# Rounded weight pairs in the expert units, and three reorderings at stage borders of a fused attention and expert kernel

## The reference, cut to what matters

```python
x = x + L0_xattn(layernorm(x), ctx)           # attention map of 256 x 256 per batch
x = x + L0_ffn(layernorm(x))                  # 8 experts, top 2, and a shared one
x = x + L1_xattn(ctx, ctx, layernorm(x))      # masked softmax of scores * layernorm(x)
x = x + L1_ffn(layernorm(x))                  # weights looked up in a table of 16 values

def L0_ffn(xt):                               # xt: 1024 x 256
    top_p, top_i = top_k(softmax(xt @ gate_w), 2)
    for k in (0, 1):                          # an expert takes up to 160 tokens per k
        h = gelu(buf @ w1 + b1)               # 256 -> 1024
        y = h @ w2 + b2 + gelu(buf @ wd) @ wu # 1024 -> 256, and rank 32
        out += y[token's slot] * keep * top_p[:, k]
    return out + 0.2 * (gelu(xt @ sw1 + sb1) @ sw2 + sb2 + gelu(xt @ swd) @ swu)

def L1_ffn(x):                                # lut[idx] are the weights
    return (silu(x @ gate.T) * (x @ up.T)) @ down.T
```

## Time and profile before

| quantity | value |
|---|---|
| median of 3 runs | 301.19 us (301.11 to 302.14) |
| profiled execution | 304.5 us, span of its instructions 302.7 us |
| PE busy | 290.1 us (96%), 1931 instructions |
| DVE busy | 243.2 us (80%) |
| ACT busy | 155.2 us (51%) |
| POOL busy | 116.3 us (38%) |
| granted PE clock | 1.000 over the whole span |

### The profile page before, as it was taken

One profiled execution on the slowest core, in us unless ns is written; L12 is line 12 of the kernel. 1 busy time (PEld: TensorE's weight loads), 2 busy tenths in 40 slices (PEclk: granted clock), 3 DMA queues, 4 the chain that ended last, 5 costly groups with the idle time before them and its releaser, 6 DMA issues.

```text
span 302.7 us, 5910 instructions
## 1 busy us (share of the span) xinstructions
PE 290.1 (96%) x1931; PEld 251.9 (83%) x1931; DVE 243.2 (80%) x647; ACT 155.2 (51%) x369; POOL 116.3 (38%) x144
## 2 busy tenths in 40 slices
PE   8988999969999999999999999999999899999895
PEld 6545688859898998989899888999888699999795
DVE  4888878848998988889888899898974778796733
ACT  2677985415554655646556555655533634535210
POOL 7527410351328074380834706051051215442431
PEclk9999999999999999999999999999999999999999
DMA  7933206550949448293573926446034000010102
GB/s 214 333 137 88 90 0 191 176 173 2 299 166 260 175 83 305 61 298 128 133 253 69 326 93 168 171 79 226 1 43 141 0 3 0 0 36 1 36 1 70
DMA packets 21858, 38.07 MB, mean 126 GB/s; under 512 B 3147, under 2 KB 12427, under 8 KB 21836
## 3 DMA queue, kind: packets, MB, share of 16 engines
q1 hardware_dynamic: 17356, 32.55, 32.6%
q0 software_dynamic: 4480, 5.25, 9.2%
HBM read 31.37 MB, written 6.42 MB: 125 GB/s over the span
## 4 chain that ended last, share of the span: by engine, by line
PE 69%; DVE 11%; ACT 7%; DMA 5%; POOL 4%; issue 3%; SPq 0%; DVEq 0%; POOLq 0%; ACTq 0%
PE hb L811 25%; PE yb L830 24%; PE yb L845 5%; PE hb L959 4%; PE tb L711 4%; DVE bst L1231 1%; POOL rstd L472 1%; DMA xg<-xnorm_dram,row_of 1%; DMA x<-xacc_dram 1%; DVE xn L1237 1%; PE rb L976 1%; DMA xacc_dram<-ysb,third_row 1%; PE yb L959 1%; ACT sm L1024 1%; DMA projw<-projw_dram 1%
## 5 line engine op out<-in xcount | busy, mean ns | idle before, releaser
L830 PE MATMUL yb<-raw,h 128*128 128x256 f32 x384 | 96.5, 379 | 1.4 <-ACT h L1137 1.4
L830 PEld LDWEIGHTS yb<-raw,h 128*128 128x128 f32 x384 | 69.1, 189 | 8.8 <-ACT h L1137 1.8
L1137 ACT ACTIVATE h<-hb,b 128x320 f32<-128x320 f32 (+1 forms) x80 | 44.6, 558 | 58.4 <-PE hb L811 57.1
L811 PE MATMUL hb<-xT_hi,w_hi 128*128 128x320 f32 (+1 forms) x180 | 71.2, 396 | 0.5 <-ACT small L1141 0.5
L811 PE MATMUL hb<-xT_lo,w_hi 128*128 128x320 f32 (+1 forms) x180 | 58.7, 326 | 0.0
L811 PE MATMUL hb<-xT_hi,w_lo 128*128 128x320 f32 (+1 forms) x180 | 58.6, 326 | 0.0
L573 POOL DMA_INDIRECT xacc_dram<-ysb,row_of x16 | 28.2, 1764 | 78.5 <-ACT ysb L1004 76.0
L1263 DVE COPY_PREDICATED pick<-bits,pick 128x544 int32<-128x544 uint8 x56 | 43.3, 773 | 0.6
L557 POOL DMA_INDIRECT xg<-xnorm_dram,row_of x24 | 28.7, 1196 | 32.5 <-DVE row_of L1535 16.3
L1648 DVE TENSOR_TENSOR w_lo<-raw,w_hi 128x256 fp32r<-128x256 f32 x84 | 34.5, 415 | 6.6 <-ACT w_hi L1004 6.5
L811 PEld LDWEIGHTS hb<-xT_hi,w_hi 128*128 128x128 f32 x180 | 33.9, 189 | 5.1 <-issue 2.2
(11 more groups left out here) (241 smaller groups left out, 513.5 us busy)
## 6 DMA issues: line engine op xcount, KB each, us to landing
raw<-w1pack_dram SPq DMA_DIRECT2D x30, 384.0 KB, 3.7
raw<-w2pack_dram SPq DMA_DIRECT2D x30, 384.0 KB, 5.4
idx<-idx_dram SPq DMA_DIRECT2D x8, 272.0 KB, 6.6
x<-x_dram SPq DMA_DIRECT2D x4, 256.0 KB, 4.3
xnorm_dram<-xn SPq DMA_DIRECT2D x2, 512.0 KB, 5.5
xacc_dram<-x SPq DMA_DIRECT2D x2, 512.0 KB, 8.3
x<-xacc_dram SPq DMA_DIRECT2D x4, 256.0 KB, 4.4
out_dram<-x SPq DMA_DIRECT2D x3, 256.0 KB, 2.1
```

Of the source, the lines that this page charges most:

```text
L811: mm = pe.matmul(hb[s % RING][:, 0:n], w[:, s, k * P:(k + 1) * P], a[:, turn, k, 0:n], start=(i == 0), stop=(i == len(terms) - 1))
L830: mm = pe.matmul(yb[c // 2][:, (c % 2) * D:(c % 2 + 1) * D], h, w, start=(s == 0 and c % 2 == 0), stop=(s == STEPS - 1), skip_group_check= ...
L1137: act.activation(hidden(s - 1, shared, turn), bank[:, 0:n], ACT.Gelu, bias=b1[:, expert, s - 1:s])\
```

## The change

- PE, end of unit 0: `second` of step 8 now stands ahead of the transposes of unit 1, and `slot_weights` behind them. `third_slots(0)` stands ahead of `second` of step 6.
- DVE, end of unit 0: `third_rows_done` stands ahead of `weight_rows`, one w1 block later than `rows_done`; `weights_done` stands behind `rows_lo` of unit 1.
- Units 2 to 8: `second` of steps 3 and 5 works with rounded pairs (`second_rounded`): three fp32r products in place of one fp32 product per 128 slots. ACT makes two rounded copies for each such step and DVE two differences. The third chunk stays as it was.
- ACT, unit 9: the exponentials of batch 1 stand behind the last gelu instead of ahead of the last two.
- DVE, the 24 rounds: `add_probs` of batch 3 is split over rounds 11 and 12 (was round 13), its `norm_x` stands in round 13 (was 14), and `finish(0)` in round 11 (was 10).

```diff
+ROUNDED = (3, 5)
@@ TensorE
+            def second_rounded(u, s, loads):
+                i = ROUNDED.index(s)
+                pe.wait_ge(pair_lo_ok, u * 4 + 2 * i - 6)
+                for c in range(2):
+                    rows = slice(c * P, (c + 1) * P)
+                    for j, (h, w) in enumerate(((h_hi, h_hi), (h_lo, h_hi), (h_hi, h_lo))):
+                        mm = pe.matmul(yb[0][:, c * D:(c + 1) * D], h[:, 2 + i, rows], w[:, i, :],
+                                       start=False, stop=False, skip_group_check=True)
+                mm.then_inc(mm2, 1)
...
+                    elif s - LAG in ROUNDED and not shared and not after_shared:
+                        second_rounded(u, s - LAG, loads)
...
             second(0, STEPS - 2, True, 0)
+            second(0, STEPS - 1, True, 0)
+            expert_rows(1, 1)
             slot_weights()
-            expert_rows(1, 1)
-            second(0, STEPS - 1, True, 0)
             third_slots(1)
@@ ScalarE
+            def pair_weights_hi(u, turn, i):
+                s = ROUNDED[i]
+                act.wait_ge(raw2_in[turn][s // 3], (u - turn) * 8 + 16)
+                act.wait_ge(mm2, u * STEPS - STEPS + s + 1)
+                copy(h_hi[:, i, :], raw2[:, turn, s, :]).then_inc(pair_hi_ok, 1)
+            def pair_rows_hi(u, turn, i):
+                s = ROUNDED[i]
+                act.wait_ge(h32_ok, u * NF + s)
+                copy(h_hi[:, 2 + i, :], hidden(s - 1, False, turn)[:, 0:S]).then_inc(pair_hi_ok, 1)
...
                         exps(1, 0)
-                        exps(1, 1)
...
+            exps(1, 1)
             x3T_copy(0)
@@ VectorE
+            def pair_lo(u, turn, i):
+                s = ROUNDED[i]
+                dve.wait_ge(pair_hi_ok, u * 4 + 2 * i - 7)
+                dve.wait_ge(mm2, u * STEPS - STEPS + s + 1)
+                dve.tensor_tensor(h_lo[:, i, :], raw2[:, turn, s, :], h_hi[:, i, :].bitcast(F32), ALU.subtract)\
+                    .then_inc(pair_lo_ok, 1)
+                dve.wait_ge(pair_hi_ok, u * 4 + 2 * i - 6)
+                dve.tensor_tensor(h_lo[:, 2 + i, :], hidden(s - 1, False, turn)[:, 0:S], h_hi[:, 2 + i, :].bitcast(F32),
+                                  ALU.subtract).then_inc(pair_lo_ok, 1)
...
                 for s in range(STEPS):
+                    if not shared and not after_shared and s in ROUNDED:
+                        pair_lo(u, turn, ROUNDED.index(s))
...
+                elif s == 4:
+                    third_rows_done()
                     weight_rows()
-                elif s == 5:
-                    third_rows_done()
-                elif s == 8:
-                    weights_done()
...
             rows_lo(3, 1, SLOTS)
+            weights_done()
             add_shared(0)
...
-                if f == 4 and b > 0:
+                if n == NG + 5 or f == 4 and b > 1:
                     finish(b - 1)
...
+                elif n == 11:
+                    add_probs(1, 3, 4, (0,))
+                elif n == 12:
+                    add_probs(1, 3, 4, (1,))
                 elif n == 13:
-                    add_probs(1, 3, 4)
-                elif n == 14:
                     norm_x(4, 3, x3n_ok)
```

More of the change, by code:

```diff
@@ L303, in program @@
         low_third_ok = sem("low_third_ok")
+        pair_hi_ok = sem("pair_hi_ok")
+        pair_lo_ok = sem("pair_lo_ok")
         up_hi_ok = sem("up_hi_ok")
@@ L868, in unit @@
                             count(1)
+                        elif s == 8:
+                            third_slots(0)
                     if s == LAG + 1:
@@ L898, in unit @@
                             slot_rows(1)
-                        elif s == 8:
-                            third_slots(0)
             def expert_rows(u, turn):
@@ L1180, in unit @@
                         split_hi(g + AHEAD, (s + AHEAD) % STEPS, u + (s + AHEAD) // STEPS)
+                    if not shared and not after_shared and s + 1 in ROUNDED:
+                        pair_weights_hi(u, turn, ROUNDED.index(s + 1))
                     if s == 6 and width:
```

3 lines of the change are left out of this document (2 added, 1 removed).

## The result

The changed kernel takes 298.5 us in the median, the kernel before 302.14 in the runs beside it (301.19 in those shown ahead): a ratio of 0.9875, 95% interval 0.9844 to 0.9905. It is faster, but by 3.6 us and not by the 5.3 of the forecast, and 298.5 lies 0.2 outside the range of 294.8 to 298.3. (In four later comparisons the changed kernel's median was 298.14, 298.48, 297.93 and 299.63, on both sides of that bound; what missed is the size of the gain.)

What follows compares the result with a forecast made beforehand. PE, busy 290.1 of 302.7 us, was taken as the bound. Gains of 2.2 + 1.3 + 1.0 + 0.8 = 5.3 us off the median of 301.19 gave 295.9 us, range 294.8 to 298.3.

Steps and rivals of the forecast that it cites:

- the last line of the sum: Whole kernel: the summed gain of 5.3 us is taken from the median of 301.19, giving 295.9.
- B: End of unit 0: later refill lets unit 1's gather land earlier, step 8 fills the wait; 1.3 us, bounds 0 and 1.4.
- C: Unit 9 on ACT: gelus no longer wait behind batch 1's exponentials; 1.0 us.
- A: Units 2 to 8: rounded pairs save PE 0.16 in each of 7 x 2 steps; 2.2 us.
- D: Rounds 10 to 14: earlier norm removes PE's 1.09 pause at batch 3; 0.8 us, bounds 0.4 and 1.0.
- The slow rival: Expert units: shared port makes differences cost 1.02, DVE becomes the bound; 309.6 us, chance 0.04 with everything else slower.
- rival 3: ACT's table switches: each costs 2.66 where it interrupts work, the unit 9 gain is gone; 296.9 us, chance 0.04.

Runs made afterwards that it cites:

- B alone: Kernel before with only the new order at the end of unit 0: 302.91 us, ratio 1.0006.
- part A alone: Kernel before with only the rounded pairs in units 2 to 8: 299.42 us, ratio 0.9908.
- C alone: Kernel before with only the exponentials of batch 1 moved behind the gelus of unit 9: 301.1 us, ratio 0.9993.
- late rows with C: Kernel before with batch 1's exponentials behind unit 9's gelus and the rows' return from DRAM delayed by a small SP transfer: 305.45 us, ratio 1.0001.
- D alone: Kernel before with only the changes to DVE's order in the 24 rounds: 301.28 us, ratio 0.9943.
- the changed kernel beside the last split: Changed kernel, no edit, timed beside the last run splitting the shared unit's last step two and two around the transposes: 299.63 us, ratio 0.9833.
- late rows and no part C: Kernel before with only the rows' return from DRAM delayed by a small SP transfer ahead of the loads of x: 304.45 us, ratio 1.0037.

## Why the prediction was wrong

**The step that failed is the last line of the sum**: "That execution was 3.3 over the median of 301.19, so I take the 5.3 from the median". It gave 295.9 where 298.5 was measured. The 3.3 was itself made of the pauses that the terms of B and C were to remove. An execution of before with neither of them can be put together from stretches of the traces: 31.01 + 34.64 + 144.27 + 29.40 + 24.88 + 34.53 = 298.7 of span, and with the 1.8 between span and time of the profiled execution (304.5 - 302.7) 300.5, where the lowest executions lie (300.3). The late gather adds 2.4, the late rows 1.6. The profiled execution had both; the median of 301.19 is only 0.7 above one with neither. Taking the full price of both off a time that hardly holds them counted them twice. How often each transfer is late was not counted; the account rests on the traces, on the lowest executions, and on the parts by themselves: taken alone, B had a ratio of 1.0006 and C one of 0.9993, nothing where 2.3 was forecast for the two, while A (0.9908) and D (0.9943) had what was forecast for them or more.

**Part A, right.** 2.0 to 2.1 for 2.2, unit 18.27 for 18.24, h_lo at 0.413 to 0.418 for 0.416, no wait before `second_rounded`, DVE at 17.64 for 17.9. The slow rival, two SBUF inputs blocked by POOL, did not come: no new difference is over 0.432. The Trainium skill (SBUF — State Buffer, "SBUF: two separate sides") has a DVE instruction with two SBUF inputs block only against a GpSimd one that reads SBUF. The row agrees as far as it goes, since POOL does nothing but issue DMAs in the units (indirect gathers and scatters); no run here puts such a POOL instruction beside a new difference.

**Part B, mechanism right, size wrong, and its sign depends.** The refill does hold the gather back, and with it later the landing comes 2.5 after the issue (B alone). But the term of 1.3 was priced at an execution in which the gather was late. In the others the reordering costs 0.7, because the chain xT_hi, xT_lo, reduction, which the forecast put at 2.1 and rightly called bare, is then compared with no wait at all. The forecast said "the reordering as such gives nothing while the rows come at 64.65: that is the point of this part". It did not ask what it gives when they come early of themselves.

**Part C, mechanism right, priced at a pause that is not always there.** The forecast was 1.0; it is worth 0.9 with late rows, 0.1 to 0.5 otherwise. Of the 1.67 in the table of stretches most is the rows coming in time in the later execution. The rule of 2.66 for a table switch (rival 3; the Trainium skill, ScalarE: Activation LUTs, "What ACT_TABLE_LOAD costs") did not show: in the changed kernel the gelu and the exponentials both start 0.02 after the end of their load, again.

```profile
231.94 1.28 ACT L1153 ACT_TABLE_LOAD   x1
233.24 0.69 ACT L1153 ACTIVATE h<-hb,b 128x512 f32<-128x512 f32 x1
...
235.58 1.28 ACT L1040 ACT_TABLE_LOAD   x1
236.88 0.60 ACT L1040 ACTIVATE sm<-sm,nmx,rstd 128x256 f32<-128x256 f32 x1
```

**Part D, undersized.** 1.4 for 0.8, past its bound of 1.0. The pause falls by 0.8 as forecast, from 1.09 to 0.31. The rest is time that the timeline does not list as idle: PE's products around `down` of round 13 stand 0.2 to 0.3 apart instead of 0.12. With part A alone, then in the changed kernel:

```profile
274.18 0.28 PE L975 MATMUL yb<-xT_lo,gw_hi 128*128 128x256 f32 x1
274.49 0.36 PE L992 MATMUL rb<-gw_hi,h_hi 128*128 128x256 f32 x1
274.68 0.29 PE L992 MATMUL rb<-gw_hi,h_lo 128*128 128x256 f32 x1
```

```profile
272.71 0.28 PE L975 MATMUL yb<-xT_lo,gw_hi 128*128 128x256 f32 x1
272.83 0.28 PE L992 MATMUL rb<-gw_hi,h_hi 128*128 128x256 f32 x1
272.94 0.28 PE L992 MATMUL rb<-gw_hi,h_lo 128*128 128x256 f32 x1
```

The first has lost 0.27 there (0.50 for two steps of 0.12, against 0.23). The other 0.3 lies at the next `down`, behind the transposes of batch 3: two of its products start 0.38 and 0.23 after the one before with part A alone (280.45, 280.83, 281.06), and 0.12 each in the changed kernel (277.97, 278.09, 278.21).

The sum over an execution without late transfers is then 2.1 - 0.7 + 0.1 + 1.4 = 2.9, and 300.3 - 297.4 = 2.9. The other 0.7 of the 3.6 is how much more often or longer the kernel before waits for late transfers; that is argued from the traces, which show the rows late only without part A.

## What to carry to other kernels

Before a pause is priced, ask what ended it. A pause that ends at a DMA belongs to one execution, and a profiled execution that lies well above the median says that it holds more of such pauses than the median does. Then subtract from the execution that has them, or weigh them by how often they occur, and work out the new order's cost for the case in which the transfer comes in time, since bare chains cost there what the wait used to hide. One trace is not enough for this: a second profiled execution of the kernel before showed one of the two pauses gone.

## What the runs showed of the hardware

POOL's third gather landed in 2.54 us or less with SP's refill held back until then, and in 4.06 to 4.27 with a refill of 384 KB pieces issued 0.5 behind it.

After a pause of PE at the end of unit 0 the granted clock fell from 1.00 to 0.50, that is from 2.4 to 1.2 GHz, in four traces (C alone, late rows with C, D alone, the changed kernel beside the last split), for 3 to 7 us. With part C alone, behind the pause of 2.34 for the gather (columns as in the line of the expert unit above):

```profile
64.00:66.00 2.00, 0.94 (x6) 0.58 (x6) 0.00 (x0) 0.00 (x0) 1.35 (x2) 1.00 0.87 283
66.00:68.00 2.00, 2.00 (x8) 1.67 (x8) 0.89 (x2) 0.77 (x2) 0.00 (x0) 0.76 0.20 66
68.00:70.00 2.00, 2.00 (x9) 1.25 (x8) 0.82 (x2) 0.00 (x0) 0.00 (x0) 0.50 0.03 8
70.00:72.00 2.00, 2.00 (x14) 2.00 (x13) 0.71 (x3) 0.91 (x3) 0.00 (x0) 0.89 0.00 0
```

`second` of step 8 takes 2.97 there instead of 1.99, and unit 1 starts 38.00 after unit 0 where the same pause without the fall gives 36.8 to 37.0. The first trace of before (2.47) and part A alone (2.26) had the pause and kept 1.00. So where the clock fell behind the pause, it cost 1 to 2.5 us more than the pause (38.00 against 36.9; 40.60 against the 38.1 that 34.64 and D alone's pause of 3.45 make). What decides whether it falls, these traces do not show.

In the trace with late rows and no part C, PE's record has slot_weights at 62.39 and the transposes at 63.25, while DVE's reduction of slot_weights starts only at 64.93 and ACT's copy at 66.38, and a pause of 1.29 stands recorded only ahead of unit 1. So a wait may be recorded behind the place where it was, and the engines that follow show it.
